# Four gate projections between the parts of P times u, in a fused attention and feed-forward kernel

## The reference, cut to what matters

```python
xn = _layernorm(x)
x = x + attn(xn) + ffn(xn)

# attn: 16 heads, keys of 16 and values of 32 elements
q, k, v = silu(causal_conv4(xn @ W))      # q and k then normalized per head
beta = sigmoid(...) * 2;  g = -exp(A_log) * softplus(xn @ a_w.T + dt_bias)
for each row t:                            # jax.lax.scan
    S = S * exp(g_t)
    delta = (v_t - k_t S) * beta_t
    S = S + outer(k_t, delta)
    o_t = q_t S
o = o * rsqrt(mean(o * o) + eps) * silu(xn @ Wgate)
attn = o @ o_w.T

# ffn: weights decoded from 4 bits; 1408 hidden columns
y = (silu(xn @ Wg) * (xn @ Wu)) @ Wd
ffn = y / sqrt(mean(y * y) + 1e-6)
```

## Time and profile before

| | us |
|---|---|
| median of 3 runs (3307.44 to 3307.93) | 3307.9 |
| the profiled execution | 3306.02 |
| its span, first to last instruction | 3304.2 |
| PE busy | 3126.4 |
| DVE busy | 2488.8 |
| POOL busy | 1924.0 |
| ACT busy | 1668.6 |

### The profile page before, as it was taken

How to read it: one execution, slowest core, us unless ns; L and a number is a source line. 1 busy time by engine, 2 the same in 40 slices (tenths; PEclk the granted TensorE clock), 3 DMA queues, 4 the chain that set the end, 5 groups by cost and what they waited for, 6 DMA issues and landing times.

```text
span 3304.2 us, 117630 instructions
## 1 busy us (share of the span) xinstructions
PE 3126.4 (95%) x45504; PEld 2246.4 (68%) x45504; DVE 2488.8 (75%) x5504; ACT 1668.6 (51%) x3338; POOL 1924.0 (58%) x2961
## 2 busy tenths in 40 slices
PE   6999999999999999999999999999999999999986
PEld 4676776676677766666767766667667666767664
DVE  7777777877777777777777778777777777777763
ACT  4544555544555544555445555445555445554442
POOL 4566555666555666556665556665556665556643
PEclk8999999999999999999999999999999999999997
DMA  3000000000000000000000000000000000000000
GB/s 119 8 21 21 5 18 21 20 21 14 10 20 21 21 21 9 15 21 21 21 21 5 18 21 21 21 15 9 21 21 21 21 9 15 21 21 21 15 2 21
DMA packets 34301, 64.95 MB, mean 20 GB/s; under 512 B 5360, under 2 KB 7152, under 8 KB 33776
## 3 DMA queue, kind: packets, MB, share of 16 engines
q1 hardware_dynamic: 29808, 52.13, 4.7%
q10 hardware_dynamic: 4096, 6.42, 0.5%
HBM read 41.76 MB, written 16.78 MB: 18 GB/s over the span
## 4 chain that ended last, share of the span: by engine, by line
PE 78%; DVE 12%; issue 7%; POOL 1%; ACT 1%; DVEq 0%; SPq 0%; DMA 0%; ACTq 0%; POOLq 0%
PE PS L1193 14%; PE PS L1146 14%; PE PS L1180 8%; PE PS L1181 7%; PE PS L1265 7%; PE PS L1405 7%; DVE arena L897 5%; PE PS L1330 3%; PE PS L1248 3%; DVE arena L984 2%; PE PS L1383 2%; PE PS L1283 2%; DVE arena L381 2%; PE PS L1301 2%; PE PS L1205 1%
## 5 line engine op out<-in xcount | busy, mean ns | idle before, releaser
L897 DVE SCALAR_TENSOR_TENSOR arena<-PS,sc,arena 128x256 f32<-128x256 f32 x2112 | 1002.9, 481 | 414.9 <-ACT arena L603 314.2
L1180 PE MATMUL PS<-xh,wgu 128*128 128x256 f32 x2816 | 904.1, 354 | 14.6 <-DVE arena L897 10.1
L1181 PE MATMUL PS<-xl,wgu 128*128 128x256 f32 x2816 | 711.2, 285 | 0.0
L603 ACT ACTIVATE arena<-PS,sc 128x256 f32<-128x256 f32 x704 | 329.7, 473 | 663.4 <-PE PS L1181 659.4
L1193 PE MATMUL PS<-wdn,inner 128*128 128x512 f32 x1408 | 656.3, 592 | 0.0
L1180 PEld LDWEIGHTS PS<-xh,wgu 128*128 128x128 f32 x2816 | 542.7, 193 | 135.0 <-issue 77.3
L1181 PEld LDWEIGHTS PS<-xl,wgu 128*128 128x128 f32 x2816 | 543.9, 193 | 97.5 <-issue 97.3
L504 POOL TENSOR_TENSOR arena<-arena,work 128x31 f32<-128x31 f32 (+15 forms) x992 | 542.6, 547 | 77.8 <-POOL work L500 0.2
L500 POOL TENSOR_TENSOR work<-arena 128x31 f32<-128x31 f32 (+15 forms) x992 | 518.8, 523 | 94.9 <-DVE arena L984 19.7
L1146 PE MATMUL PS<-xnT,wqkv 128*128 128x256 f32 x2048 | 491.1, 391 | 9.5 <-ACT inner L583 9.5
L1146 PEld LDWEIGHTS PS<-xnT,wqkv 128*128 128x128 f32 x2048 | 383.2, 193 | 76.0 <-issue 13.6
(11 more groups left out here) (153 smaller groups left out, 4753.0 us busy)
## 6 DMA issues: line engine op xcount, KB each, us to landing
xt<-in_x SPq DMA_DIRECT2D x64, 256.0 KB, 3.3
obuf<-in_x SPq DMA_DIRECT2D x64, 256.0 KB, 2.7
out<-obuf SPq DMA_DIRECT2D x64, 256.0 KB, 2.0
wqkv<-in_wqkv ACTq DMA_DIRECT2D x1, 2048.0 KB, 14.2
arena<-in_gup ACTq DMA_DIRECT2D x2, 704.0 KB, 6.2
arena<-in_dns SPq DMA_DIRECT2D x1, 1408.0 KB, 11.9
wg<-in_wg ACTq DMA_DIRECT2D x1, 1024.0 KB, 20.6
wo<-in_wo ACTq DMA_DIRECT2D x1, 1024.0 KB, 17.2
```

Source lines behind the costliest of these rows:

```text
L603: eng.activation(fa[:, u % 4, :], PS[:, bank(u, 0), 0:NB * P], ACT.Copy, scale=sc[:, u % 2, KB * m:KB * m + 1]).then_inc(fa_scaled.sem, 1)
L897: eng.scalar_tensor_tensor(out=fa[:, u % 4, :], in0=PS[:, bank(u, k // 2), k % 2 * NB * P:][:, 0:NB * P], scalar=sc[:, u % 2, KB * m + k:K ...
L1180: eng.matmul(o, w, xh[:, k, :], start=True, stop=False)
L1181: ins = eng.matmul(o, w, xl[:, k, :], start=False, stop=True)
```

## The change: what it does

On PE the four parts of the second gate projection leave their place behind the grams. Each now stands ahead of a part of P times u. Unit 1 moves behind the last part of P times u and ahead of the grams, unit 2 behind the grams, right ahead of unit 3. `turn_q` stands behind part 1. On DVE `gram_products` now comes ahead of unit 2. On ACT the gate copy comes ahead of the copies of P times u, unit 1 behind them, and unit 2 behind the squares. On POOL the two operations of `layer_norm_scale` move behind the clearing of the solve's array.

The waits follow: the gate's first part waits for the masked keys (bank 6), unit 1 for the gate copy (same bank), `turn_q` for the scaled queries themselves.

```diff
@@ pool_step
-                if more:
-                    layer_norm_scale(eng, n.next())
                 next_tile(eng, t, n)
                 keys_for_state(eng, t, n)
                 clear_solution(eng, n)
+                if more:
+                    layer_norm_scale(eng, n.next())
@@ act_step
             queries()
-            unit(1)
+            gate_copy(1)
             if t:
                 eng.wait_ge(*pu_out.at(t, 1))
                 for b in range(NB):
                     eng.activation(by_pair(sq[:, b, :]), paired(1, b), ACT.Copy).then_inc(o_copied.sem, 1)
-            unit(2)
+            unit(1)
...
             eng.wait_ge(*taps_done.at(n, NQKV))
+            unit(2)
             eng.activation(qkv[:, 4:NQKV, :], qkv[:, 4:NQKV, :], ACT.Silu).then_inc(silu_done.sem, 1)
-            gate_copy(1)
             unit(3)
@@ half_unit, u == 1, half 0
-                        eng.wait_ge(*knq_copied.at(n, 2 * NB))
+                        eng.wait_ge(*gate_copied.at(n, NB))
@@ gate, b == 1
-                        eng.wait_ge(*fa_done.at(n, 2))
+                        eng.wait_ge(*knq_copied.at(n, 2 * NB))
@@ turn_q
-                eng.wait_ge(*qk_kept.at(n, NB))
+                eng.wait_ge(*qk_done.at(n, NB))
                 if t:
                     eng.wait_ge(*ku_masked.at(t, NB * NC))
+                else:
+                    eng.wait_ge(*qk_kept.at(n, NB))
@@ pe_step
+            gate(1, 0)
             p_times_u(0)
+            gate(1, 1)
+            p_times_u(1)
             turn_q()
-            p_times_u(1)
+            gate(1, 2)
+            p_times_u(2)
+            gate(1, 3)
+            p_times_u(3)
             unit(1)
-            p_times_u(2)
-            p_times_u(3)
-            unit(2)
             gram(0)
             gram(1)
-            for kb in range(KB):
-                gate(1, kb)
+            unit(2)
             unit(3)
```

## The result

| | before | after |
|---|---|---|
| median, us | 3307.9 (3307.4 to 3310.8, 4 runs) | 3338.3 (3338.0 to 3338.7, 4 runs) |
| ratio | 1 | 1.0091 [1.0075, 1.0107] |
| span of the profiled execution | 3304.2 | 3336.2 |
| mean granted clock | 0.974 | 0.986 |

The changed kernel is slower by 30 us; forecast were 26. The later runs were made on other chips of the same kind, on which the kernel before took 3315.9, 3320.4 and 3322.0 us. So each of them is given as a ratio to the kernel before on its own chip. On the last of these chips the changed kernel was run once more and stood at 1.0064 [1.0050, 1.0077].

A forecast was written before the change was run, and what follows sets the result against it. PE, busy 95%, was bound by the fetch pause in P times u, then DVE's chain; 8.2 + 18.05 = 26.25 against 25.5 us, 0.8 a step, 26 us over 32 steps, gave 3334 us (range 3302 to 3370).

The forecast's parts named there:

- The pause is the instruction fetch: P times u on PE: the 1.6 us pause is the fetch of 16 KB blocks, about 3.6 us apart; shrinks to 0.6.
- First part: Start to end of P times u on PE: 8.2 us, against about 7.7 in the mean step before; bounds 8.0 and 9.9.
- Second part: End of P times u to half 1 of unit 8, through ACT and DVE: 18.05 us against 17.81, 0.25 longer.
- Sum: Both parts of a step together: 26.25 us against 25.5, so 0.8 us slower a step.
- The clock: If the steps' clock drops stay, compare with the step without one: 1.5 us a step slower, 48 us in all, 3356.
- rival 4: Half clock over the wide gate matmuls behind the pause: 1.2 us a step more than the forecast, 3372; chance 0.12.
- The waits: L1330's issue wait falls from 60 to about 20 us, the grams' vanishes, L1180 waits 55 to 65 for L1005.
- What costs nothing: `layer_norm_scale` moved on POOL: 0; rows scaled later: 0, at most 0.2 us a step through DVE; new `turn_q` wait: 0.

The follow-up runs named there:

- Experiment 3: Kernel before with 40 more semaphore instructions on PE in the first step only: runs between 3365.5 and 9775.9 us, no ratio; the profiled one 3366.3 us.
- experiments 7 and 8: Changed kernel with `layer_norm_scale` ahead of the state's keys again on POOL: 1.0074; then side by side, changed kernel 1.0064, with POOL's order of before 1.0063.
- Experiments 1, 2 and 9: 1: changed kernel, DVE's gram products behind unit 2 again, 1.0330. 2: changed kernel, unit 2 ahead of the grams on PE, ACT, DVE, 1.0289. 9: see experiment 9.
- experiment 9: Kernel before with all four gate parts among P times u, units and DVE order kept, other banks for units 1 and 2: 1.0146.
- banks only: Kernel before with nothing moved, only unit 1 in banks 4 and 5 and unit 2 in 7 and 4: 1.0007.

## Why the prediction was right, point by point

- **The pause is the instruction fetch.** Experiment 3 shows that it is tied to the place in the instruction stream, and the packets of the fetch's queue end 1.4 us ahead of each end of a pause. The 3.6 us between blocks, which the forecast took from three pauses, is about right: the packets of the earlier trace rows start 3.44 and 3.57 us apart, and the least distance of two is 3.24 us before and 3.25 in the changed kernel. In the changed kernel the pause stands behind 55 records (56 forecast). One reading beside it was wrong, though nothing hung on it: narrow matmuls would use up a block (127 matmul records from pause to pause) in 1.3 and not 2 us, by the 83 in 0.84 of the earlier trace rows.
- **First part, 8.2 us to the end of P times u.** In the step above, 8.25: without the gate part 0 would have begun at 2696.51, 0.36 us behind the start of the last product of queries and state as before, and P times u ended at 2704.76. The pause was 0.46 there (0.6 forecast) and there is no second one, as forecast. The first gate part began 0.18 late, at 2696.69; forecast was 0.2. In the mean of 30 steps this part took 8.46 us, against 7.61 before, half clock behind the pause included (forecast 8.2 against 7.7): the pause is 0.46 to 1.02 us, 0.66 in the mean.
- **Second part, 18.05 us.** Measured 17.77 (2722.53 - 2704.76), where 17.81 stood before. DVE started unit 1 at 1.52 (1.6), the products ended at about 6.0 (6.0), PE stood still 1.59 (1.9). Sums ended at 8.7 (8.9). The forecast was 0.3 too long here. In the mean it was 17.79, against 17.70 before.
- **Sum.** 0.8 forecast, 0.95 measured from the start of L989 to the next. It is 0.85 from the first part (0.5 forecast) and 0.09 from the second (0.25 forecast). The errors have opposite signs, so that the sum came this near is in part luck; the mechanism and both signs were right.
- **The clock.** Step against step without half clock the loss is 1.5 us in the two steps shown (100.91 against 99.41), as the text gave it, and 1.4 in the mean (101.16 against 99.75). What makes it 0.95 over all is mostly that steps with half clock fell from 23 to 6 of 30. The forecast had this only inside the mean step of before. Half clock over the gates (rival 4) did not appear: all six stretches begin 0.1 to 0.6 us after PE's wait ahead of unit 3 has ended.
- **The waits.** "Issue" at L1330: 22.5 (about 20). Grams: 1.6 in one place (none). L1180 for L1005: 52.2 in 32 places (55 to 65). Idle ahead of L1004: gone. All as stated.
- **What costs nothing.** POOL's order: shown by experiments 7 and 8. The later scaling of the rows: DVE waited 100.0 us for POOL's result ahead of L989, where before it was 67.2, which is 1.0 us a step where 0.2 at most was forecast. But it did not reach PE: from half 1 of unit 8 to the end of the step PE takes 37.0 us in both kernels, and to the next step's last product of queries and state 74.7 in the mean of both.
- **What my account lacked, though it did no harm here.** I took DVE's queue as the only thing that sets the chain behind P times u. Experiments 1, 2 and 9 show that this holds only while PE's wait ahead of unit 3 stays short: at 1.6 us it is hidden and the clock mostly stays; at 2.6 us 23 of 30 steps lose clock; at 4.1 us all do and unit 3 comes late to DVE. It lacked also the meeting of hidden with POOL. That half clock follows such a wait is read from the traces; that it alone makes up the rest of the loss in experiment 9 was not separated from the meeting with POOL.

Where the time went, then: the stretch to the end of P times u took in four gate parts, gave up unit 1 and most of its pause, and became 0.85 us longer in the mean. The stretch behind it gave up those gate parts, 3.1 us of PE's work, for unit 1, about 1 us, and did not become shorter (17.70 to 17.79), because DVE's chain sets it and the gates had only covered PE's wait for the gram products.

## What to carry to other kernels

One wide gate part of 1.06 us ahead of the narrow matmuls did not lessen what PE waits for the fetch (69 of 72 us), but cut it into shorter pauses, behind which the clock stayed up, and that was the gain (0.4%). All four brought that wait down to 24 us, but each gate part beyond the first left the wait ahead of unit 3 with less to cover it (0, 0.7, and 2.6 us a step with one, two and four). Before moving work off a place, ask what PE waits for there once it is gone, and for how long, since a long wait is followed by half clock. Order what DVE owes PE first and its own backlog behind, so that PE's next result is made while DVE is busy.

## What the runs showed of the hardware

- **DVE and POOL in each other's way.** A 128x256 operation of DVE with both inputs in SBUF takes 0.43 us, and 1.15 to 1.27 us when it starts just behind the start of a 128x512 operation of POOL (1688.41 and 1688.58 above; the row shows two such operations, 1.05 us the first). What it costs is what is left of POOL's operation less 0.15 us: at 1688.58 about 0.88 were left, and 0.73 were added. The Trainium skill ("SBUF — State Buffer", section "🔬 SBUF: two separate sides") says that the two share one pair of ports, and that whoever starts first holds it for its whole instruction, for DVE operations with two SBUF inputs too when POOL's operation reads SBUF. The trace agrees. A shift of 0.8 us in an earlier stage was enough to make them meet.
- **The instruction fetch in narrow matmuls.** Blocks of 16 KB start no less than 3.2 us apart in every trace here, and PE goes on from a pause in P times u 1.4 us after one has landed (1.40 to 1.46 in the mean of each trace).
- **Placement of instructions.** Forty instructions once, far ahead of the steps, cost about 50 us in the run that can be read, through a new pause in every step.
- **Chips differ.** The kernel before took 3307.9 on one chip and 3315.9 to 3322.0 on others, and the ratio of the changed kernel moved from 1.0091 to 1.0064. Part of it is the fetch: its packet takes 1.02 us in the mean in the trace of before on the first chip and 1.12 in that of banks only on another, and PE's waits put down to "issue" sum to 79.4 and 93.1 us, 13.7 more, where the kernel before took 12.4 us longer on that chip. In the changed kernel, which has fewer such pauses, they sum to 30.2 and 34.8 us on two chips, which fits its lower ratio there. The kernel before was not profiled on the other chips, so this is read from kernels that differ in their banks. Intervals of one chip say nothing of this, so close kernels must run side by side.
